# Mixture-of-experts stage: all sixteen experts for every token, or sorted tiles of the four chosen

## The reference

```python
logits = x @ router_weight.T + router_bias          # 1024 tokens, 16 experts
top_val, top_idx = jax.lax.top_k(logits, 4)
router_scores = zeros.at[arange(T)[:, None], top_idx].set(softmax(top_val))
gate_up = einsum('th,ehd->etd', x, gate_up_proj) + gate_up_proj_bias   # 256 -> 512
gate = minimum(gate_up[..., ::2], 7);  up = clip(gate_up[..., 1::2], -7, 7)
out = einsum('etd,edh->eth', (up + 1) * gate * sigmoid(1.702 * gate), down_proj) + down_proj_bias
out = (out * router_scores.T[:, :, None]).sum(axis=0)
```

## Time and profile before

| | us |
|---|---|
| median of 3 runs | 1080.28 (1079.12 to 1080.34) |
| span of the profiled execution | 1077.1 |
| PE busy | 1014.8 (94%) |
| DVE busy | 856.1 (79%) |
| ACT busy | 619.1 (57%) |
| POOL busy | 556.3 (52%) |
| stage B on PE, first to last expert matmul | 40.7 to 341.1 |

### The profile page before, as it was taken

The page is one execution under the profiler, slowest core; times in us unless marked ns, Lnnn a source line. Parts: engine busy times, 40 slices in busy tenths (PEclk is TensorE's granted clock), DMA queues, the critical chain, the costliest instruction groups (busy, mean ns, idle before and its releaser), DMA issues. The chain is left out here.

```text
span 1077.1 us, 19032 instructions
## 1 busy us (share of the span) xinstructions
PE 1014.8 (94%) x6538; PEld 865.3 (80%) x6538; DVE 856.1 (79%) x2154; ACT 619.1 (57%) x1661; POOL 556.3 (52%) x409
## 2 busy tenths in 40 slices
PE   8999999999999899889867999999999999999988
PEld 6458888888888677556546888998899988999976
DVE  6467777776778867789988898879888898878885
ACT  1774444444333246888556657775677657776643
POOL 4247666668653233135246565656555555655550
PEclk9999999999999999999989999999999999999999
DMA  7002101010100011000001101010100101000201
GB/s 273 1 18 97 60 30 59 31 59 30 59 1 28 1 57 49 32 2 2 21 1 31 49 1 41 1 60 1 40 1 22 40 1 40 1 21 1 90 1 40
DMA packets 15007, 37.43 MB, mean 35 GB/s; under 512 B 1648, under 2 KB 6848, under 8 KB 14400
## 3 DMA queue, kind: packets, MB, share of 16 engines
q1 hardware_dynamic: 14912, 36.21, 9.9%
HBM read 35.16 MB, written 1.05 MB: 34 GB/s over the span
## 5 line engine op out<-in xcount | busy, mean ns | idle before, releaser
L2343 ACT ACTIVATE y<-bank,g_mx 128x256 f32<-128x256 f32 x256 | 117.2, 484 | 115.7 <-DVE g_mx L2526 115.7
L2627 POOL TENSOR_TENSOR y<-y,g_sm 128x1024 f32<-128x1024 f32 x64 | 119.9, 1893 | 25.4 <-DVE g_sm L2542 25.4
L2603 POOL TENSOR_TENSOR g_c<-arena 128x1024 fp32r<-128x1024 f32 x30 | 64.0, 2133 | 112.4 <-DVE arena L2447 112.4
L2216 PE MATMUL bank<-arena 128*128 128x256 f32 x512 | 116.3, 380 | 0.0
L795 ACT ACTIVATE arena<-arena 128x512 f32<-128x512 f32 x64 | 40.4, 632 | 120.6 <-DVE arena L880 120.5
L2216 PEld LDWEIGHTS bank<-arena 128*128 128x128 f32 x512 | 94.9, 190 | 12.0 <-issue 0.2
L743 PE MATMUL bank<-b_yh,b_wh 128*128 128x512 f32 x256 | 100.6, 393 | 0.0
L743 PE MATMUL bank<-b_yl,b_wh 128*128 128x512 f32 x256 | 100.0, 390 | 0.0
L743 PE MATMUL bank<-b_yh,b_wl 128*128 128x512 f32 x256 | 99.7, 389 | 0.0
L831 POOL TENSOR_TENSOR b_hl<-arena,b_hh 128x512 fp32r<-128x512 f32 x64 | 81.3, 1291 | 9.6 <-ACT b_hh L804 9.6
L2099 PE MATMUL bank<-cst,y 128*128 128x128 f32 x512 | 71.9, 274 | 11.0 <-POOL y L2627 6.3
(11 more groups left out here) (387 smaller groups left out, 3111.4 us busy)
## 6 DMA issues: line engine op xcount, KB each, us to landing
arena<-in_dram SPq DMA_DIRECT2D x37, 512.0 KB, 3.6
arena<-in_dram SPq DMA_DIRECT2D x18, 256.0 KB, 3.9
arena<-in_dram SPq DMA_DIRECT2D x3, 1024.0 KB, 5.0
arena<-in_dram SPq DMA_DIRECT2D x2, 704.0 KB, 7.3
x<-in_dram SPq DMA_DIRECT2D x4, 256.0 KB, 4.7
cx<-in_dram SPq DMA_DIRECT2D x4, 256.0 KB, 5.1
cxT<-in_dram SPq DMA_DIRECT2D x4, 256.0 KB, 5.7
cx<-in_dram SPq DMA_DIRECT2D x1, 1024.0 KB, 7.9
```

Source lines behind the costliest of these rows:

```text
L2216: m = pe.matmul(o[:, st * 256:st * 256 + 256], g_t[:, c, st * P:st * P + P], keys, start=True, stop=True)
L2343: m = act.activation(g_p[:, c, st, :], o[:, st * 256:st * 256 + 256], ACT.Exp, bias=g_mx[j % 2][:, 2 * c + st:2 * c + st + 1], accum_out=g ...
L2603: pool.tensor_tensor(cat, g_o[j % 2], g_om, ALU.subtract).then_inc(s_gc, 1)
L2627: pool.tensor_tensor(pf, pf, sums, ALU.mult).then_inc(s_gp, 1)
```

## The change

Stage B now computes only (token, expert) pairs that are chosen, 4096 of them. DVE and PE make a table at run time: the mask is counted per expert over the tokens before (`rank`, two matmuls against constants), each expert gets ceil(count / 128) tiles of 128 slots, at least one, and each pair a slot. At most 47 tiles are needed, and 47 are always computed. One-hot matrices (`b_oneA`, `b_oneB`) and 32 small matmuls (`table`) turn this into a list of the token of each slot (`b_idx`); `experts_dve` makes the place of each tile's weights (`b_et`).

The normed rows are stored to DRAM (`b_rows_d`, DMAs issued by ACT). For each tile POOL issues an indirect DMA that fetches 128 rows; PE transposes them, adds the bias by a matmul that picks a bias row (`b_sel`), and multiplies them with the expert's weights, whose address it loads into a register. These matmuls have the 128 slots as stationary operand and 512 (down: 256) weights moving, in plain f32 with no split; the hidden values are transposed by PE for the down matmuls. Results go to DRAM (`b_slots_d`), and after the last tile POOL fetches each token's four rows back by 32 indirect DMAs, and DVE adds them, scaled by the scores. All weights stay in SBUF: 11 experts are loaded at the start, five once the routing's work area is free.

All sixteen key projections now come before the first tile, and the sixteen key transposes behind the last.

```diff
         def B_pe(pe):
+            for n in range(4, 7):
+                K_raw_pe(pe, n)
+            rank()
+            for n in range(7, 13):
+                K_raw_pe(pe, n)
+            table(range(0, 4))
+            K_raw_pe(pe, 13)
+            table(range(4, 8))
+            K_raw_pe(pe, 14)
+            K_raw_pe(pe, 15)
+            def gate_up(j, at_):
+                o = claim(pe, ("B", "gu", j))
+                pe.matmul(o[:, :], b_sel[:, j:j + 1].to_broadcast([P, P]), b_bias[:, :], start=True, stop=False)
+                have(pe, ("B", "xT", j))
+                for k in range(KD):
+                    m = pe.matmul(o[:, :], b_xT[j % 2][:, k, :], arena[:, bass.ds(at_ + 512 * k, 512)],
+                                  start=False, stop=(k == KD - 1))
+                fill(m, ("B", "gu", j))
+            pe.wait_ge(s_bet, 2)
+            expert = {}
+            rows_T(0)
+            for s_ in range(NTL + 2):
+                if s_ + 1 < NTL:
+                    rows_T(s_ + 1)
+                if s_ < NTL:
+                    expert[s_] = pe.value_load(b_et[0:1, s_:s_ + 1], min_val=0, max_val=W_AT[NE - 1])
...
+                    gate_up(s_, expert[s_])
...
+                if 1 <= s_ <= NTL:
+                    hidden_T(s_ - 1)
+                if s_ >= 2:
+                    down(s_ - 2, expert[s_ - 2])
+            for n in range(NK):
+                K_tr_pe(pe, n)
         def B_pool(pool, C):
-            split_e_pool(pool, 0)
             ctx_quant_pool(pool, C)
             K_rstd_pool(pool, C, 0)
             K_rstd_pool(pool, C, 1)
+            pool.wait_ge(s_byst, 16 * B)
+            pool.wait_ge(s_bidx, 1)
+            for j in range(NTL):
+                if j >= NR:
+                    take(pool, ("B", "xT", j - NR))
+                pool.indirect_dma_start(b_xg[j % NR], None, b_rows_d,
+                                        bass.IndirectOffsetOnAxis(ap=b_idx[:, j:j + 1].bitcast(U32), axis=0))\
+                    .then_inc(s_bxg[j % NR], 16)
...
+        def B_back_pool(pool, b):
+            if b == 0:
+                for n in range(3):
+                    pool.wait_ge(s_bst[n], 16 * len(range(n, NTL, 3)))
+            for n in range(2 * TOPK * b, 2 * TOPK * b + 2 * TOPK):
+                pool.indirect_dma_start(b_back[:, n, :], None, b_slots_d,
+                                        bass.IndirectOffsetOnAxis(ap=b_pi[:, n:n + 1].bitcast(U32), axis=0))\
+                    .then_inc(s_bk[b], 16)
         def B_dve(dve, V):
+            bias_dve(dve, V)
+            mask_dve(dve, V)
+            dve.wait_ge(s_bc, 16)
+            place_dve(dve, V)
+            V.do(dve.tensor_scalar(b_pi.rearrange("p (t k) -> p t k", k=TOPK), b_p8[:, :, 0:TOPK], -1.0, None, ALU.add))
+            scores_dve(dve, V)
+            o = take(dve, ("B", "table"))
+            V.sync()
+            empty(dve.tensor_copy(b_idx, o[:, 0:NTP]), ("B", "table"))
...
+            experts_dve(dve, V)
+            setup_dve(dve, V)
+            slot_scores_dve(dve, V)
+            G_consts_dve(dve, V)
         def M_dve(dve, V, done):
             for b in LOW:
+                B_combine_dve(dve, V, b)
+                ln_open_batch(dve, V, b)
                 ln_scale(dve, K_C, b)
                 C_quant_dve(dve, V, b)
...
-            B_last_dve(dve, V)
+            for b in HIGH:
+                B_combine_dve(dve, V, b)
         def M_pool(pool, C):
-            ln_pool(pool, C, K_C, EPS, batches=LOW)
+            B_back_pool(pool, 0)
+            B_back_pool(pool, 1)
+            ln_pool(pool, C, K_C, EPS, batches=(0,))
+            B_back_pool(pool, 2)
+            ln_pool(pool, C, K_C, EPS, batches=(1,))
+            B_back_pool(pool, 3)
```

More of the change, by code:

```diff
@@ L23 @@
 I32 = mybir.dt.int32
+U32 = mybir.dt.uint32
 ALU = mybir.AluOpType
@@ L67 @@
 NCST = 314
+ROUTE_AT = NCST + 512 + SLOTS
+ROUTE = {"iota": (0, 128), "below": (128, 256), "ones": (256, 384), "tile": (384, 432), "token": (432, 440), "lane": (440, 441)}
+NROUTE = 441
+NTL = T * TOPK + NE - 1
+NTP = NTL + 1
+W_EXP = KD * (4 * P) + KD * D
+W_LOW = 11
+W_AT = [e * W_EXP + (1664 if e >= W_LOW else 0) for e in range(NE)]
 YT_AT = 41500
@@ new lines, in down_bias @@
+            def down_bias(c):
+                o = claim(pe, ("B", "bd", c))
+                have(pe, ("B", "sT", c // 2))
+                for j in range(2):
+                    t = 2 * c + j
+                    m = pe.matmul(o[:, j * D:j * D + D], b_sT[0:NE, t * P:t * P + P], b_bd[0:NE, :],
+                                  start=True, stop=True)
+                fill(m, ("B", "bd", c))
+            for n in range(4, 7):
[3 more added lines that the diff above has]
+                K_raw_pe(pe, n)
@@ new lines, in hidden_T, with down @@
+            def hidden_T(j):
+                o = claim(pe, ("B", "hT", j))
+                pe.wait_ge(s_bh, j + 1)
+                for k in range(KD):
+                    m = pe.transpose(o[:, k * P:k * P + P], b_u2[j % 2][:, k * P:k * P + P], ident)
+                fill(m, ("B", "hT", j))
+            def down(j, at_):
+                o = claim(pe, ("B", "dn", j))
+                have(pe, ("B", "hT", j))
+                for k in range(KD):
+                    m = pe.matmul(o[:, 0:D], b_hT[j % 2][:, k, :], arena[:, bass.ds(at_ + 1024 + D * k, D)],
+                                  start=(k == 0), stop=(k == KD - 1))
+                fill(m, ("B", "dn", j))
@@ L768, in B_act @@
+            for n in range(NK):
+                K_tr_pe(pe, n)
+        s_btu = sem("b_one_hots_used")
         def B_act(act):
@@ new lines, in hidden_T, with gelu, out @@
+            def hidden_T(j):
+                if j >= 2:
+                    take(act, ("B", "dn", j - 2))
+                o = take(act, ("B", "hT", j))
+                empty(act.copy(b_hT[j % 2], o[:, 0:2 * P].rearrange("p (k n) -> p k n", k=KD)), ("B", "hT", j))
+            def gelu(j):
+                act.wait_ge(s_bgt, j + 1)
+                act.activation(b_g[j % 2], b_g[j % 2], ACT.Gelu_apprx_sigmoid).then_inc(s_bt, 1)
+            def out(j):
+                o = take(act, ("B", "dn", j))
+                if j >= 3:
+                    act.wait_ge(s_bst[j % 3], 16 * (j // 3))
+                empty(act.copy(b_o[j % 3], o[:, 0:D]), ("B", "dn", j))
@@ L810, in B_pool @@
+            rows_T(0)
+            for s_ in range(NTL + 2):
+                if s_ + 1 < NTL:
+                    rows_T(s_ + 1)
+                if 1 <= s_ <= NTL:
+                    hidden_T(s_ - 1)
+                if s_ < NTL:
+                    gelu(s_)
+                if s_ >= 2:
+                    out(s_ - 2)
+                if D_FIRST <= s_ < D_FIRST + NI:
+                    D_split_act(act, s_ - D_FIRST)
+            for n in range(NK):
+                K_tr_act(act, n)
         def B_pool(pool, C):
-            split_e_pool(pool, 0)
```

558 lines of the change are left out of this document (275 added, 283 removed).

## The result

The changed kernel takes 1038.76 us (median of 4 runs, 1036.45 to 1041.6) against 1080.11 us for the kernel before (4 runs of the same chip, 1079.12 to 1080.34): a ratio of 0.9618 with an interval of 0.9596 to 0.9639, some 41 us less. The forecast was 1011 us. The profiled execution of the changed kernel spans 1039.8 us; before it was 1077.1. So 37.3 us were gained where the working had 69.5, and 32.2 us are missing.

What follows compares the result with a forecast made beforehand. PE's matmul columns were taken to bound the expert stage. The last quantising step was to gain 76.0 us, less 5.0 for moved sums and 1.5 for clock, net 69.5: 1077.1 - 69.5 + 3.2 = 1010.8 us, range 978 to 1062.

Steps and rivals of the forecast that it cites:

- The new start: Stage B's start: routing table, context reduction and POOL's queue put the first gate/up at 72.9 us, not 40.7.
- 62.0 + 0.4 + 2 x 3.1 = 68.6 us: POOL at the start: context reduction's end, all-reduce, then two key rstds, after which the first gather is issued.
- 3.25 us by their columns: Tile loop: PE's matmuls and transposes sum to 3.25 us a tile; 3.4 taken, for waits between short groups.
- 2 for the clock: First tiles: 2 us added for a clock that may have fallen while PE was idle for ten us.
- The register: Tile loop: loading each weight address into a PE register, taken as 0, with 1.2 us a tile (56 us) as other end.
- Rival (a): Tile loop: PE waits at each tile for its register, 0.9 us a tile, 42 us: 1053 us; chance 0.15.
- 1.2 us each: POOL: the cost of issuing one gather, 47 for the tiles and 32 to bring results back.
- Rival (b): Start and end: a gather costs POOL up to 2.9 us, 25 stand bare, 43 us: 1054 us; chance 0.15.
- rival (d): Tile loop: POOL becomes the bound; gain used up at 3.6 us a gather, 1109 us at 4; chance 0.09.
- Rival (c): POOL's gathers: DVE slows them 1.5 times, to 1.8 us, 15 us in all: 1026 us; chance 0.06.
- 5.0 us for the moved sums: Before stage D: sums of batches 2 and 3 (6.6 us) replace four additions (1.63 us), giving 5.0 us back.
- (e): Gathers and tiles: a gather costs only 0.43 us (-19 us), tiles 3.25 us (-7): 985 us; chance 0.09.

Runs made afterwards that it cites:

- run 1: Changed kernel with the two key square roots moved ahead of the all-reduce on POOL, gathers still behind it: 1030.13 us.
- run 2: Changed kernel with two key square roots, then the first four gathers, moved ahead of the all-reduce on POOL: 1030.19 us.
- run 3: Changed kernel with the all-reduce replaced by a copy on POOL, so context scales are per partition: 1032.6 us.
- run 9: Changed kernel with DVE's reduction of the context's largest values moved from behind the experts' table to behind the mask, POOL's order kept: 1020.43 us.
- run 10: On top of run 9, additions of batches 2 and 3 moved behind stage D's first scaling, batch 3's last two gathers behind D's first square root: 1015.58 us.
- run 4: Changed kernel with weight addresses as constants, no register load or register arithmetic; tiles use wrong experts: 1038.44 us.
- run 5: Changed kernel with 39 tiles instead of 47, enough for these inputs: 1014.63 us.
- run 11: On top of run 10, each batch's return gathers counted in two halves, first-half additions started early, POOL's square roots moved earlier: 1007.48 us.
- run 12: Run 10 with only the counting of run 11: each batch's gathers on two semaphores, four each, order unchanged: 1010.29 us.
- run 7: Changed kernel with 512 instead of 1024 bytes of scratch for POOL's DMA descriptors: 1047.92 us.
- run 6: Changed kernel with 16 instead of 32 return gathers, each fetched row added twice: 1022.97 us.
- run 8: Changed kernel with dummy matmuls (38, 20 and 18) on PE ahead of the first transposes of stages C and D: 1038.31 us.

## Why the prediction came out as it did

The change did what the working said, in each place where work was counted, and missed time in the places where an engine stands. The misses, from the profiled execution, sum to the 32.2 us: +16.2 up to the first gate/up, +3.4 in the loop, +8.8 from its end to the last quantising step, +3.7 and -0.9 up to stage D, +1.0 behind it.

**The new start, 72.9 against 89.11.** The logits were at 37.75 (forecast 37.6) and the places at 49.4 (49.3). Then the first mis-sized term: the 32 one-hots at 0.17 us each took 8.45 us, 0.26 each:

```profile
49.64 8.45 DVE L985 TENSOR_SCALAR b_oneB<-arena 128x128 fp32r<-128x128 f32 x32
```

This is 3.0 of the 4.4 us by which the reduction of the context came late. The step that failed was the next one, "62.0 + 0.4 + 2 x 3.1 = 68.6 us": it names POOL's queue, which was right, and sums the busy times of what stands in it, which was not. From the reduction's end to the first gather it took 17.1 us, not 6.6, of which 9.35 are the stand and 1.2 the all-reduce itself (1.05 where I had 0.4) with small gaps. Runs 1, 2, 3 and 9 tie it to the all-reduce: moved with it, gone without it, free where POOL has nothing else to do. The rest (1.3 us) is in the first gather, its landing and the transposes.

The Trainium skill (GPSIMD Engine Reference, "2.1 Instruction dispatch") states that the first call to a freshly loaded GpSimd routine pays some 6 us behind a change of the pool's configuration, with no instruction of its own in the profile. The trace agrees in kind and shows it somewhat longer: the stand begins at such a change, and measured 9.35, 7.21, 7.14 and 7.01 us in four kernels, and 6.71 before. That it is paid both into the all-reduce and out of it is what run 2 adds.

**The tiles.** 3.25 us by their columns was right (3.26 measured); the 0.15 us that I put on top for waits was not needed, which is 6.0 us over the last 43 tiles. Against it, the first four took 24.5 us (89.11 to 113.65) and not 13.6 with 2 for the clock. Run 10 has the same instructions at a granted clock of 1.00, in 19.2 us. Of these I had left out the score transposes and bias matmuls (5.0 us: 1.04 + 1.99 + 1.99) and two waits for DVE (2.75 us); the first tiles have less of their own, having no earlier tile's down matmuls. The other 5.4 us, where I had 2, go with the clock: 0.50 up to 90 us, 0.58 to 94, and again 0.70 and 0.50 from 102 to 110. That is a term of the working mis-sized by 3.4 us, and only for executions like this one: runs 4 and 5 lost 1.2. 8.9 - 6.0 and a late tile of 0.5 us make +3.4.

**The register.** Taken as 0, and 0 it is: from the fifth on the tiles are the same distance apart with and without it (run 4). The trace of the changed kernel has the load itself:

```profile
L782 PEldq TENSOR_LOAD <-arena x47: 296/307/512, 88.0 to 248.7; - x47
```

It takes 0.31 us, under the cover of queued matmuls; the 0.42 us on issue ahead of the first tile (none in run 4) is all that shows of it. Rival (a) is dead. The Trainium skill's floor of some 600 ns (DMA: Bandwidth & Descriptors, "Latency and other measured facts"), quoted in the prediction, is twice what this load measured, so the measurement decides; covered, both come to the same.

**The gathers.** 1.2 us each was close: 0.95 and 0.30 to the next, 1.25. Rival (b) and the slower rival (d) needed 2.9 and 3.6 us. Rival (c), 1.5 times slower beside DVE, did not come either: the longest single one took 1.77 us. The spread that spoke for it was weaker than I read it: at 71.53 in the kernel before, the same subtraction took 2.38 us beside a DVE that was busy throughout (3.00 of 3.00 us from 71 to 74), about as short as alone. What I hadn't foreseen is the gap ahead of each eighth gather, which makes the mean 1.5 us. Sixteen gathers from 259.83 end at 283.93, 24.1 us instead of 19.2: +4.9. The next eight had their gap too: the second square root ended at 298.8, 13.7 us behind the first, where the working had 10.5: +3.2. The chain and the store of the last tile took 0.6 more. That is the +8.8.

**The way to stage D.** 5.0 us for the moved sums was the right term with a wait left out: DVE stood 3.19 us for the last gather. I had sized the sums and not asked when their rows would be there, the same fault as at the start. The 1.5 us for a fallen clock was 0.6.

**The range.** 1038.76 lies inside 978 to 1062, and it is none of the cases that I had priced: the nearest by time were (c), 1026, and (a) and (b), 1053 and 1054, and their mechanisms were all absent. Of (e) half came, the tiles at 3.25 us, while a gather cost 1.25 and not 0.43. So the range held by luck, for another reason than the ones it was made of. The signs say the same: the first gate/up was due at 70 to 76 us and came at 89.1, the last quantising step at 275 and came at 303.8. The working had warned of another operation ahead of the gathers on POOL, but as a wait for DVE, not as a stand of POOL's own. That runs 11 and 12 reach about 1011 us, with the all-reduce's stands covered and the gaps gone, doesn't confirm the working either, since its misses went both ways.

What stays open: why the gap goes with the count on a semaphore and with the scratch at once. Runs 7 and 12 show both, and a rule that joins them was not tried. Nor was a larger scratch. Why the clock of the first tiles is at one level in some executions and at the other in others, behind the same work, is open too; that it also makes the two pairs among the changed kernel's own times is likely (4.8 us between them) but not shown, since one of the four was profiled. And nothing explains why the stand is 8.3 to 9.4 us in the six profiled executions with the changed kernel's order on POOL, and 6.6 to 7.3 in the others.

## What to carry to other kernels

When a change uncovers a stretch of an engine's queue, read the idle times of that stretch in the old trace, not only the durations: a stand that was free under other work is priced in the old profile (6.71 us there, 9.35 here). When a queue grows new members, ask of each what it can be late for, and look for a hole earlier in another engine's queue before re-ordering the slow one: a 2.28 us instruction moved into a 2.39 us wait gained more than either re-ordering on POOL. And if an experiment succeeds by the amount expected, look in its trace whether it did so for the reason expected: in run 11 a gap had gone that nothing was meant to touch, and in run 10 a clock had done half of what the move was credited with.

## What the runs showed of the hardware that was not expected

- POOL's all-reduce across partitions took 0.4 to 1.05 us itself, but cost 8.6 us of standing ahead of it where POOL came from gathers (run 2), and 6.6 to 9.4 us behind it, until the next tensor instruction (all kernels but run 3's). A gather behind it started after 0.21 us (run 1).
- An indirect DMA of 128 rows of 1 KB took POOL 0.95 us, 0.30 us apart. The eighth in a row on one semaphore was held 2.3 us with 1024 bytes of scratch (changed kernel); with 512 bytes it was the fourth and the seventh (run 7). With four in a row on a semaphore none was held in 32 (run 12), nor in 16 (run 6).
- A register load from SBUF in PE's queue took 0.31 us and cost nothing behind 3.26 us of queued matmuls.
- The granted clock of 0.65 to 0.72 in the stretches with waits was worth no more than the measurement can tell (run 8).
- The same first four tiles took 24.1 us in run 9 and 19.2 in run 10. They started at the same time behind the same work, once at a granted clock of 0.57 and once at 1.00.
- From issue to landing the first nine gathers took 2.6 to 6.6 us (run 2). The DMA engines' share was up to 1.05 there, with weights still being loaded.
